# A layer with a mixture of experts: the second layer's weights read in whole rows, its output summed in two halves

## The reference

```python
xn = layernorm(x)
# attention-like part: running sums over the tokens of each sequence
k_real, v = xn @ Wk, xn @ Wv                      # 1024 x 1024 each
k = exp(1j * 10 * k_real);  rot = exp(1j * t * freqs)
pos   = real(cumsum(v * rot) * conj(rot)) / sqrt(t + 1)
assoc = real(cumsum(v * conj(shift(k))) * k) / sqrt(t + 1)
a = (pos * gate0 + assoc * gate1) @ Wo
# mixture of 8 experts, one expert per token
p = softmax(xn @ gate_w);  e = argmax(p);  w = p[e]
h = gelu(xn @ w1[e] + b1[e])                      # 1024 -> 4096
y = h @ w2[e] + b2[e]                             # 4096 -> 1024
out = x + a + w * y
```

## Time and profile before

| | |
|---|---|
| runs, median (lowest to highest) | 1154.43 us (1152.5 to 1196.57), 3 runs |
| the profiled execution | 1152.25 us |
| its span, first to last instruction, on the slowest core (4) | 1150.4 us |
| spans of the 8 cores | 1135.3 to 1150.4 us |
| busy: TensorE / VectorE / ScalarE | 81% / 66% / 52% |
| HBM read, written | 321.18 MB, 17.90 MB |

### The profile page before, as it was taken

How to read it: one execution, slowest core, us unless ns; L and a number is a source line. 1 busy time by engine, 2 the same in 40 slices (tenths; PEclk the granted TensorE clock), 3 DMA queues, 4 the chain that set the end, 5 groups by cost and what they waited for, 6 DMA issues and landing times.

```text
span 1150.4 us, 18743 instructions; the slowest of 8 cores (1135.3 to 1150.4 us)
## 1 busy us (share of the span) xinstructions
PE 932.1 (81%) x6221; PEld 611.9 (53%) x6296; DVE 756.4 (66%) x1909; ACT 598.4 (52%) x1014; POOL 162.6 (14%) x184
## 2 busy tenths in 40 slices
PE   3756689699989999988889978987898784978592
PEld 2323456465656666656556646654665462544261
DVE  4726444756645546689976998999989995321331
ACT  4354477668875795576347634873377422210000
POOL 0000121001112111121012101210121110311101
PEclk9876689999989999999899988998899887988896
DMA  8999999995999999999999999999999999999982
GB/s 190 228 204 205 203 158 172 163 158 106 164 139 160 181 179 162 159 174 169 159 176 170 169 156 175 173 163 159 159 164 167 158 156 196 210 230 217 203 230 79
DMA packets 123779, 199.69 MB, mean 174 GB/s; under 512 B 4755, under 2 KB 70691, under 8 KB 123680
## 3 DMA queue, kind: packets, MB, share of 16 engines
q0 software_dynamic: 107056, 151.65, 88.8%
q1 hardware_dynamic: 16624, 46.80, 12.6%
HBM read 321.18 MB, written 17.90 MB: 295 GB/s over the span
## 4 chain that ended last, share of the span: by engine, by line
PE 33%; DVE 22%; issue 18%; DMA 18%; ACT 7%; POOL 1%; DVEq 1%; SPq 0%; ACTq 0%; POOLq 0%
PE yb L935 10%; DMA yg<-ys,gidx 10%; PE wb L621 9%; PE wb L880 8%; DVE pp L723 6%; DMA ring<-w 5%; PE yb L406 3%; DVE pp L729 2%; DVE pp L726 2%; DVE pp L749 1%; DVE pp L677 1%; DVE m L655 1%; PE wb L582 1%; DVE st L340 1%; DMA resf<-xown 1%
## 5 line engine op out<-in xcount | busy, mean ns | idle before, releaser
L880 PE MATMUL wb<-xsT,ring 128*128 128x288 bf16 x2048 | 275.4, 293 | 32.1 <-DMA ring<-w 14.6
L935 PE MATMUL yb<-hT,ring 128*128 128x288 bf16 x2048 | 283.3, 294 | 18.7 <-ACT yT L950 16.5
L880 PEld LDWEIGHTS wb<-xsT,ring 128*128 128x128 bf16 x2048 | 202.6, 100 | 100.7 <-issue 37.2
L935 PEld LDWEIGHTS yb<-hT,ring 128*128 128x128 bf16 x2048 | 204.0, 100 | 90.5 <-issue 26.7
L315 POOL DMA_DIRECT2D ring<-w x128 | 106.1, 832 | 778.9 <-PE yb L935 381.1
L890 ACT ACTIVATE hT<-wb,cfs 128x288 bf16<-128x288 f32 x256 | 118.5, 501 | 100.9 <-PE wb L880 100.1
L650 ACT ACTIVATE cs<-cs 128x512 f32<-128x512 f32 x64 | 40.3, 630 | 116.4 <-DVE cs L644 115.9
L667 DVE COPY cs<-bnd 128x2 f32<-128x2 f32 x64 | 11.1, 173 | 135.1 <-ACT cs L652 134.1
L621 PE MATMUL wb<-xT,wks 128*128 128x512 bf16 x339 | 87.1, 398 | 12.3 <-ACT hT L890 9.7
L621 PE MATMUL wb<-xT,wvs 128*128 128x512 bf16 x383 | 93.0, 386 | 0.1
L723 DVE TENSOR_TENSOR_SCAN pp<-pp,cpos,one 128x256 f32<-128x256 f32 x128 | 88.9, 736 | 3.8 <-DVE pp L729 0.5
(11 more groups left out here) (151 smaller groups left out, 1288.4 us busy)
## 6 DMA issues: line engine op xcount, KB each, us to landing
ring<-w POOLq DMA_DIRECT2D x128, 1024.0 KB, 22.1
xt<-xown SPq DMA_DIRECT2D x16, 512.0 KB, 8.2
xt<-xfh SPq DMA_DIRECT2D x16, 512.0 KB, 10.0
resf<-xown SPq DMA_DIRECT2D x16, 512.0 KB, 13.6
out<-resf SPq DMA_DIRECT2D x16, 512.0 KB, 9.1
xr<-xnb SPq DMA_DIRECT2D x16, 256.0 KB, 9.6
yg<-xr SPq DMA_DIRECT2D x16, 256.0 KB, 7.6
ys<-xsr SPq DMA_DIRECT2D x7, 576.0 KB, 10.6
```

Of the source, the lines that this page charges most:

```text
L880: fn = lambda e, kt=kt, b=b, a=a, k=k: e.matmul(b[:, 0:CAP], ring[k][:, (kt % 4) * DM + a * P:(kt % 4) * DM + (a + 1) * P], xsT[:, kt * CA ...
L935: fn = lambda e, d=d, kc=kc, k=k: e.matmul(yb[d][:, 0:CAP], ring[k][:, (kc % 8) * CH + d * P:(kc % 8) * CH + (d + 1) * P], hT[:, kc * CAP: ...
```

## The change

Second layer's loads. Each of the 8 loads of `w2` now takes 4 blocks of 128 rows by all 1024 columns, that is whole rows of 4 KB in DRAM, instead of 8 blocks by 512 columns. Size and number stay.

Order of stage 2. With such loads a buffer holds both halves of the columns. The hidden width is cut in two halves `u`, and the quarters go (u, h) = (0, 0), (0, 1), (1, 1), (1, 0). The right half's sums stay in PSUM over the second and third quarter. The left half's sums of the first quarter are written by ScalarE, with the bias, to `ypart` in float32, and after the fourth quarter VectorE adds them to the four banks into `yT`. A buffer is freed in the second quarter that reads it.

Around it. The right half is now complete first, so `y_rows(e, 1)` stands at step 53 of stage 2, and `y_rows(e, 0)` with the store moves to `ct` 12 of the next stage 1 (5 for the last expert), `load_xs` to `ct` 15. In expert 7 the projection begins after `ct` 6. `ypart` takes SBUF: `resf` has 11 buffers instead of 13. `yg` has 6 instead of 4, four of them over `xT`. `add_rows` follows two rows behind, not one.

The core of the diff:

```diff
@@ constants
-NRES = 13
-NYG = 4
+NRES = 11
+NYG = 6
@@ buffers
-    yg = [sb("yg%d" % k, DM, BF16)[0] for k in range(NYG)]
-    fxn = yg[2:]
+    ypart, _ = sb("ypart", 4 * CAP)
+    fxn = [sb("fxn%d" % k, DM, BF16)[0] for k in range(2)]
+    yg = [sb("yg%d" % k, DM, BF16, xT_off + 2048 * k)[0] for k in range(NYG - 2)] + fxn
@@ pieces
-        for h in range(2):
-            for q in range(4):
-                pieces.append((ap(w2, e_ * DFF * DM + q * KT * P * DM + h * CH,
-                                  [[DM, P], [DM * P, KT], [1, CH]]), KT, CH))
+        for q in range(8):
+            pieces.append((ap(w2, e_ * DFF * DM + q * 4 * P * DM,
+                              [[DM, P], [DM * P, 4], [1, DM]]), 4, DM))
@@ wo_part
-            if i > 0:
+            if i > 1:
+                add_rows(i - 2)
+            if i == NLT - 1:
                 add_rows(i - 1)
-            if i == NLT - 1:
                 add_rows(i)
@@ stage2
+        for s, (u, h) in enumerate(((0, 0), (0, 1), (1, 1), (1, 0))):
+            for c in range(NCT // 2):
+                kc = u * (NCT // 2) + c
+                n = e_ * 16 + 8 + kc // 4
                 k = n % NRING
+                first, end = c == 0 and s != 2, c == NCT // 2 - 1 and s != 1
+                used = s in (1, 3) and kc % 4 == 3
...
+                if used:
                     feed(t_m)
+                if end:
                     for d in range(4):
                         m = 4 * h + d
+                        part = ypart[:, d * CAP:(d + 1) * CAP]
+                        to = yT[:, m * CAP:(m + 1) * CAP]
+                        if s < 3:
+                            t_e = S.op(lambda e, d=d, m=m, to=(to if s else part): e.activation(
+                                to, yb[d][:, 0:CAP], AF.Identity,
+                                bias=cf[:, B2 + e_ * KT + m:B2 + e_ * KT + m + 1]),
+                                yd_t[d], yTr_t.get(h) if s else part_t[0])
+                        else:
+                            t_e = V.op(lambda e, d=d, to=to, part=part: e.tensor_tensor(
+                                to, yb[d][:, 0:CAP], part, ALU.add),
+                                yd_t[d], yTr_t.get(h), part_in)
+                        yb_free[d] = t_e
@@ the experts
+        at_y = 12 if e_ < NE - 1 else 5
         if e_ > 0:
-            fix.append((2, lambda e_=e_: (y_rows(e_ - 1, 1), store_y(e_ - 1, y_d))))
+            fix.append((at_y, lambda e_=e_: (y_rows(e_ - 1, 0), store_y(e_ - 1, y_d))))
         if e_ == NE - 1:
-            fix.append((2, lambda: (fetch_rows(0, y_d), fetch_rows(1, y_d))))
+            fix.insert(0, (at_y, lambda: (fetch_rows(0, y_d), fetch_rows(1, y_d))))
         else:
-            fix.append((9, lambda e_=e_: load_xs(e_ + 1)))
+            fix.append((at_y + 3, lambda e_=e_: load_xs(e_ + 1)))
+        lead = 0 if e_ < NE - 1 else at_y + 1
-            fix = [(NCT + 5, lambda e_=e_: y_rows(e_, 0)),
+            fix = [(53, lambda e_=e_: y_rows(e_, 1)),
-    last_rows(1)
+    last_rows(0)
```

More of the change, by code:

```diff
@@ L927, in store_y @@
         xsr_free[0] = (d_ys.tok(),)
+    part_t = [None]
     def stage2(e_, at_kc):
-        for h in range(2):
-            for kc in range(NCT):
-                n = e_ * 16 + 8 + h * 4 + kc // 8
+        for s, (u, h) in enumerate(((0, 0), (0, 1), (1, 1), (1, 0))):
+            for c in range(NCT // 2):
+                kc = u * (NCT // 2) + c
+                n = e_ * 16 + 8 + kc // 4
                 k = n % NRING
+                first, end = c == 0 and s != 2, c == NCT // 2 - 1 and s != 1
+                used = s in (1, 3) and kc % 4 == 3
@@ L934, in stage2 @@
                 for d in range(4):
-                    fn = lambda e, d=d, kc=kc, k=k: e.matmul(
+                    fn = lambda e, d=d, kc=kc, k=k, h=h, first=first, end=end: e.matmul(
                         yb[d][:, 0:CAP],
-                        ring[k][:, (kc % 8) * CH + d * P:(kc % 8) * CH + (d + 1) * P],
-                        hT[:, kc * CAP:(kc + 1) * CAP], start=(kc == 0), stop=(kc == NCT - 1))
-                    if kc == NCT - 1 or (d == 3 and kc % 8 == 7):
+                        ring[k][:, (kc % 4) * DM + (4 * h + d) * P:
+                                (kc % 4) * DM + (4 * h + d + 1) * P],
+                        hT[:, kc * CAP:(kc + 1) * CAP], start=first, stop=end)
@@ L940, in stage2 @@
+                    if end or (d == 3 and used):
                         t_m = T.op(fn, ring_tok[n], h_t[kc])
-                        if kc == NCT - 1:
-                            yd_t[d] = t_m
-                    else:
-                        T.quiet(fn, ring_tok[n], h_t[kc], yb_free[d] if kc == 0 else None)
-                if kc % 8 == 7:
+                        yd_t[d] = t_m
+                    else:
+                        T.quiet(fn, ring_tok[n], h_t[kc], yb_free[d] if first else None)
@@ L956, in stage2 @@
+                        yb_free[d] = t_e
+                    if s == 0:
+                        part_in = t_e
+                    else:
+                        yT_t[h] = t_e
+                for fn in at_kc.get(s * (NCT // 2) + c, ()):
                     fn()
+        part_t[0] = t_e
         hT_free[0] = t_m
@@ L1168, in more @@
             stage1(e_, {})
-            stage2(e_, {NCT + 5: [lambda e_=e_: y_rows(e_, 0)]})
-            y_rows(e_, 1)
+            stage2(e_, {53: [lambda e_=e_: y_rows(e_, 1)]})
+            y_rows(e_, 0)
             store_y(e_, ym_d)
```

26 lines of the change are left out of this document (12 added, 14 removed).

## The result

The changed kernel takes 1177.45 us (median of four runs, 1176.6 to 1178.12) where the kernel before took 1153.47 (median of four) on the same chip: a ratio of 1.021, with a 95% interval of 1.0184 to 1.0235. It is slower by 24 us. The prediction said 1151, with a range up to 1176. The profiled execution took 1176.6 us, and its slowest core, number 2, spans 1175.1.

The account below looks back on a forecast made before the run. It took PE, then DVE (experts 3 to 6), as the limit, with little spare in the weight stream and a tail short of DMA time. Terms -4 -4 +5 +3 +4 -2 -3 = -1 from 1152.25 gave 1151 us, range 1124 to 1176.

Parts of the forecast that it names:

- What bounds the kernel: PE in expert 2, DVE with PE close behind in experts 3 to 6, DMA time in the tail; stream little to spare.
- The rows: 4 KB rows make second-layer loads faster, 0.36 to 0.70 us each: -4 us in experts 2 and 3, -4 in the tail.
- (a) The fourth load: Stage 2: needed at step 12, not 24, 5 us before landing in experts 2 to 4; +5 us, between 0 and +15.
- (b) The hole: Stage 2: no load issued for 16 steps, but the queue has work until 574.5 and the next load just fits; 0 us.
- PSUM boundaries: Stage 2 stops for eviction after steps 15, 47 and 63 instead of 31 and 63; +3 us over eight experts, at most +12.
- The sums on DVE: 32 new sums adding the halves, 500 ns each, half hidden in DVE's idle time in experts 3 to 6; +4 us.
- ScalarE (-2): ScalarE has 4 x 508 ns less to do before the first hT of seven experts, PE gains perhaps 0.3 us each; -2 us.
- The tail: Expert 7 with the output projection: store and gathers 5 us earlier, closing a 3 us hole; buffers worth 0; -3 us.
- Rival 3: Bunched ring: late seventh or eighth load stalls PE, 4 us per expert, 1180 us; sign over 25 us at steps 40-48; chance 0.14.
- Rival 4: DVE sums and boundaries at their upper ends (+8, +12), the rest as summed (-8): 1164 us; chance 0.16.

Follow-up runs that it names:

- e13: Control: the kernel before with six of the eight row blocks in each second-layer load (a quarter of w2 not transferred); 0.990 of the kernel before.
- e2: The changed kernel with each second-layer load issued as two transfers of 2 KB rows instead of one of 4 KB rows; 1180.84 us, 1.0261 of the kernel before.
- e9: The changed kernel with two of four row blocks in the third and fourth second-layer load of each expert; 1.0094 of the kernel before.
- e1: The kernel before with stage 2's loads issued when the changed kernel issues them (after steps 19 to 31 and 51 to 63); 1156.83 us, 1.007 of the kernel before.
- e3: The changed kernel without the eviction of the left half's first sums after step 15 (a tile of zeros is added instead); 1.0055 of the kernel before.
- e7: The changed kernel with a unit due between steps 10 and 15 of stage 2 issued right after step 15, behind the eviction; 1.0107 of the kernel before.
- e11: As e3, and ScalarE does the left half's last eviction instead of a sum on DVE; 1.0009 of the kernel before.
- e5: The kernel before with six gather buffers, 11 output tiles and row sums two rows behind; 0.9985 of the kernel before.
- e6: As e5, and in expert 7 row transposes, store and first gathers stand after ct 5 instead of 2, the projection after them; 0.9966 of the kernel before.
- e14: The changed kernel with the edits of both e3 and e8; 0.9826 of the kernel before.
- e8: The changed kernel with three of four row blocks in every second-layer load (a quarter of w2 not transferred); 0.9995 of the kernel before.

## Why the prediction was wrong, step by step

- **What bounds the kernel: right.** DVE leads in experts 3 to 6, PE waits behind it, and the stream has little to spare: by e13 a quarter of the second layer's bytes is worth only 1.0% of the kernel before.
- **The rows (-8): right in kind.** Engine time per MB fell to 6.2 us, a little below the 6.47 taken; about 6 us by e2, with overlapping intervals. Not all of it came where it was counted: the ring waits went up, not down.
- **(a) The fourth load (+5): too small.** It took 5 us in each of three experts, 15, less what falls away in stage 1. On core 2 the waits at steps 4 to 15 are 31.1 us, in experts 2 to 7. In stage 2 of expert 2 alone they cost 7 us by e9, with only 5.3 us of waiting on core 2: the 20 matmuls behind it took 5.59 us where they take 2.61 at full clock. What the prediction set against it is real: the 14.6 us of ring waits in the stage 1 of experts 3 and 4 are gone but for 0.2 on core 4, and these stages are 3.8 and 6.2 us shorter there (51.8 and 51.9 us).
- **(b) The hole (0): this step failed, and by its own working.** It took 5 us and 20 steps at 0.85 us, 22 us in all. The durations of the steps were sound: in e1 the same 20 steps with both units take 17.2 us, and there the queue indeed has work throughout. But the boundary after step 15 lies inside these 20 steps, and I priced it in another paragraph as if it were elsewhere. With it DVE's pace comes in: in experts 3 to 5 the wait for `ypart` ends 26.4 to 27.3 us after the stage began on every core, late load and low clock or not. In e1 the wait behind the same sines ends after 26.4 us as well, but there the load has been issued 9 us earlier. So the first load goes out after 32 us and not after 22, the queue stands empty for some ten microseconds, and the eighth load lands after step 44 is due. The prediction also followed only the seventh load. By its own figures the eighth would have landed 6.7 us behind it, at 588, with step 44 due at 544.1 + 5 + 44 x 0.85 = 586.5. What the hole costs by itself no run isolates.
- **PSUM boundaries (+3): this term failed most.** "The boundary after 15 inherits" the old wait of 4.1 us was an argument by likeness, with an upper end of 12. The order rows showed what was missing: a unit of step 13 is recorded just ahead of the eviction, and its sines need a DVE that is still at the last unit. Before, row transposes lay ahead of the boundary after step 31. On the eight cores the wait became 6.5 us in expert 0, 6.2 to 12.0 in expert 3, 2.7 to 6.0 in expert 4 and 3.0 to 9.1 in expert 5, and the price 18 us by e3, 12 of them by the place of one unit (e7).
- **The sums on DVE (+4): right.** 448 ns each (row below) for the 500 taken, and 5 us by e11 against e3.

```profile
L967 DVE TENSOR_TENSOR yT<-yb,ypart x32: 444/448/458, 275.0 to 1157.1; 128x288 bf16<-128x288 f32 x32
```

- **ScalarE (-2): not priced by any run.** The shorter stage 1 of experts 3 and 4 is no sign of it, since the ring waits that went from there are larger than the gain.
- **The tail (-3): right in size by e5 and e6 (2 to 4 us), wrong in its way.** In the changed kernel the gathers did not come earlier. GpSimd on core 2:

```profile
973.48 0.74 POOL L315 DMA_DIRECT2D ring<-w  x1 [1.22 <-PE yb L944]
1016.45 1.03 POOL L811 DMA_INDIRECT yg<-ys,gidx  x1 [42.23 <-DMA ys<-xsr]
```

The first gather starts 43.6 us after expert 7 began; in the trace of before it was 36.1 (951.8 to 987.94), with the waits of the earlier trace rows around it. `y_rows` stands 14.2 us for DVE's sum, where I had taken 2: this sum too is behind DVE's last body. The store takes 20.17 us of the chain. From the start of expert 7 to the end of the span it is 202.3 us on core 2 and 199.8 on core 4, and was 198.6: here the tail lost 1 to 4 us.
- **Rival 3, with 0.14, came nearest**: 1180 against 1177, with waits of 4.47 and 5.41 us at step 44 in two experts. That is partly luck. Its sign was over 25 us of ring waits at steps 40 to 48, and core 2 has 15.9 there; and it named the bunched ring as sufficient, which e1 refutes, and had nothing of the boundary. Rival 4 had the boundary at +12, not at 18. What happened is a mixture of both, and I had no case with both. Splitting by e13, e14 and e8: 0.7% faster without the two, 1.7% for the boundary, 2.1% less the 1.0% that the kernel before has as well for the stream, together 2.1%. That they add up is no check, since the four ratios multiply back to 1.021 by the way they are formed; the check is that the boundary costs 1.5% with the full loads and 1.7% with the lighter ones.

**What stays open.** Why in each pair one core's loads land too late for steps 40 to 47 and the other's don't. The hole is some 32 us long on both, so both issue into an empty queue. No run here changed one core alone. Nor does any run split the stream's 1.1% between the hole and the early fourth load beyond expert 2.

## What to carry to other kernels

A stretch in which no buffer comes free must be priced with everything that stands inside it: every wait and every boundary, in one sum; a cost that is booked in another line is missing there. If one of these waits ends when another engine is through, that engine's time is the length of the stretch, and the terms before it don't add. When an eviction gets a new place, read what is ahead of it in its engine's queue at that place, and not what an old boundary cost. And test with the control: fewer bytes helped the kernel before as well, and only the difference spoke of the change.

## What the runs showed of the hardware

- Two neighbouring cores, one load: in the profiled run the gaps of the pairs are 20.0, 19.2, 23.0 and 21.8 us, and in the other three runs of the changed kernel it is partly the other core of a pair that is late. e8 has such gaps too (1136.5 and 1121.2 us). The Trainium skill (HBM Reference, Specifications (TRN2)) says that two cores of a domain share its bandwidth; that would fit pairs whose loads restart after an empty queue, and waits at steps 40 to 47 of 12.7 to 15.9 us on one core and 1.6 to 4.3 on the other, but no run here isolates it.
- In expert 2, on core 2, waits of 1.43 and 3.83 us were followed by 20 matmuls in 5.59 us, which took 2.61 at a granted clock of 1.00; the clock was 0.83 in 439.5 to 460 us and 1.00 after it. PE is the limit there, so the 3 us were lost on top of the waits. In expert 3 a clock of 0.84 and 0.77 ahead of the eviction cost nothing: DVE sets when PE goes on, and a slower PE only stood 6.22 us there instead of core 4's 10.24.
- 4 KB rows took 6.2 us of engine time per MB, 2 KB rows 7.14 in the kernel before and 7.04 in e2, at the same number of bytes landed.
